# Four residual blocks on eight images: x(1) loaded when x(0) is there, other orders in the first and last cycle, and x2 of images 0 and 7 copied from SBUF to C's windows

## What is computed

```
x = x + conv3x3(gn(x), w0) + b0          # A, zero padding
x = x + inverse(gn(x))                   # B
x = x + circular_conv3x3(gn(x), w2)      # C, wraps around in rows and columns
x = x + mask * conv3x3(gn(x), K)         # D, last row and column of the conv are 0

def inverse(W):                          # each channel is a 128 x 128 matrix
    X = W^T / (norm1 * norminf)          # the norms are maxima over the channels of an image
    for _ in range(5):                   # Newton-Schulz
        X = X @ (2 I - W @ X)
    return X
```

## Time and profile before

| | |
|---|---|
| median of 3 runs | 651.18 us (649.93 to 652.49) |
| profiled execution, its own time | 653.21 us |
| its span | 651.1 us, 12738 instructions |
| TensorE busy, matmuls / weight loads | 595.6 us (91%) / 505.6 us (78%) |
| VectorE | 509.9 us (78%) |
| ScalarE | 357.9 us (55%) |
| GpSimd | 192.0 us (29%) |
| mean granted TensorE clock | 0.974 of full |
| DMA | 69.07 MB, 106 GB/s on average |
| share of the chain that ended last: TensorE, VectorE | 80%, 8% |

### The profile page before, as it was taken

How to read it: one execution, slowest core, us unless ns; L and a number is a source line. 1 busy time by engine, 2 the same in 40 slices (tenths; PEclk the granted TensorE clock), 3 DMA queues, 4 the chain that set the end, 5 groups by cost and what they waited for, 6 DMA issues and landing times.

```text
span 651.1 us, 12738 instructions
## 1 busy us (share of the span) xinstructions
PE 595.6 (91%) x3880; PEld 505.6 (78%) x3880; DVE 509.9 (78%) x1477; ACT 357.9 (55%) x713; POOL 192.0 (29%) x283
## 2 busy tenths in 40 slices
PE   0596996999999999999999999999999999988775
PEld 0475985798879787889779787889879887987454
DVE  2877587789887898888887898798887888598660
ACT  0354524575567557575558547566558447643452
POOL 6020440054214240154114241254014041440303
PEclk9998997999999999999999999999999999997888
DMA  6154113227334344236414544426414324400432
GB/s 171 49 152 119 50 51 120 63 51 226 94 91 93 116 137 143 82 82 182 153 54 99 145 137 119 112 64 194 131 52 104 107 81 134 108 33 34 134 107 65
DMA packets 85859, 69.07 MB, mean 106 GB/s; under 512 B 7886, under 2 KB 77166, under 8 KB 84910
## 3 DMA queue, kind: packets, MB, share of 16 engines
q1 hardware_dynamic: 80768, 63.21, 34.3%
q0 software_dynamic: 3456, 4.63, 2.7%
q10 hardware_dynamic: 1598, 0.77, 0.5%
HBM read 31.84 MB, written 25.30 MB: 88 GB/s over the span
## 4 chain that ended last, share of the span: by engine, by line
PE 80%; DVE 8%; DMA 3%; ACT 3%; SPq 3%; issue 2%; POOL 0%; DVEq 0%; ACTq 0%
PE conv_ps L628 40%; PE R_ps L775 17%; PE V_ps L775 16%; PE R_ps L736 4%; SPq L276 2%; DMA win_A<-x 2%; PE conv_ps L753 1%; PE V_ps L753 1%; DMA x<-x_dram 1%; DVE st L563 1%; DVE bn_A L444 1%; ACT DN L907 1%; ACT d_C L543 1%; DVE VT L1062 1%; PE row_ps L769 0%
## 5 line engine op out<-in xcount | busy, mean ns | idle before, releaser
L628 PE MATMUL conv_ps<-d_C,w_C 128*96 128x512 f32 (+1 forms) x486 | 112.6, 389 | 7.8 <-POOL d_C L674 6.9
L628 PEld LDWEIGHTS conv_ps<-d_C,w_C 128*96 128x96 f32 x486 | 76.0, 166 | 39.2 <-issue 10.2
L628 PE MATMUL conv_ps<-d_A,w_D 128*96 128x512 f32 (+1 forms) x432 | 102.2, 387 | 2.0 <-DVE w_D L496 2.0
L1254 POOL TENSOR_TENSOR RC<-RY 128x512 f32<-128x512 f32 x32 | 40.4, 1283 | 171.3 <-ACT RY L891 171.3
L628 PE MATMUL conv_ps<-d_A,w_A 128*96 128x512 f32 (+1 forms) x378 | 88.7, 390 | 2.0 <-DVE w_A L496 2.0
L628 PEld LDWEIGHTS conv_ps<-d_A,w_D 128*96 128x96 f32 x432 | 66.2, 164 | 25.4 <-DVE w_D L496 2.1
L674 POOL TENSOR_TENSOR d_C<-d_C,ones_all 128x8 fp32r<-128x8 f32 (+1 forms) x96 | 26.0, 302 | 190.1 <-DVE d_C L506 190.0
L628 PEld LDWEIGHTS conv_ps<-d_A,w_A 128*96 128x96 f32 x378 | 59.4, 167 | 24.2 <-DVE w_A L496 2.1
L663 ACT ACTIVATE out_C<-conv_ps,col_C 96x512 f32<-96x512 f32 (+1 forms) x48 | 31.1, 648 | 60.0 <-PE conv_ps L628 60.0
L663 ACT ACTIVATE out_D<-conv_ps,col_D 96x508 f32<-96x508 f32 (+1 forms) x48 | 30.8, 641 | 59.1 <-PE conv_ps L628 57.6
L775 PE MATMUL R_ps<-RY 128*128 128x128 f32 x512 | 62.1, 277 | 0.5 <-ACT RY L891 0.5
(11 more groups left out here) (179 smaller groups left out, 1170.2 us busy)
## 6 DMA issues: line engine op xcount, KB each, us to landing
win_C<-rows_dram SPq DMA_DIRECT2D x40, 256.0 KB, 3.9
x<-x_dram SPq DMA_DIRECT2D x16, 512.0 KB, 4.6
rows_dram<-x SPq DMA_DIRECT2D x32, 256.0 KB
y<-out_D SPq DMA_DIRECT2D x160, 48.0 KB
win_D<-out_C SPq DMA_DIRECT2D x7, 1056.0 KB, 6.8
x_dram<-out_A SPq DMA_DIRECT2D x35, 192.0 KB, 2.9
win_A<-x SPq DMA_DIRECT2D x79, 64.0 KB
win_A<-x POOLq DMA_DIRECT2D x56, 64.0 KB, 2.9
```

The costliest lines, as they stand in the source:

```text
L628: return pe.matmul(conv_ps[g % 2][0:OP, 0:kn, :], c.w[:, wp, dx * OP:(dx + 1) * OP], c.d[:, dp, k0:k0 + kn, dx:dx + W], start=(wp, dp, dx) ...
L1254: pool.tensor_tensor(RC[s][:, :, :], RY[s][:, :, :], RY2[s][:, :, :], ALU.add).then_inc(s_half, 1)
```

## The change

- **Start.** Image 0's windows go over the queues as groups 0 and 3 (SP), 1 and 4 (ScalarE's), 2 and 5 (GpSimd's), with four semaphores of their own, so that VectorE's statistics begin with groups 0 to 2. All three queues then wait until image 0 has landed (`x0_loaded`) before they load image 1. The bias is loaded ahead of that wait; the taps of C and D come behind it.
- **x2 of images 0 and 7.** `windows_from_x2` takes the place of stores, edge rows and loads in cycles 0 and 7. Each of the 22 windows is one DMA from 8 (at the edges 7) partitions of x2 to 128 (112) of `win_C`, and two more DMAs bring the wrapped rows. SP issues the first half of each group and GpSimd the second, 12 DMAs each, when the whole of x2 is there. They have a semaphore per group and queue, for which `high_parts` waits.
- **First cycle.** `dve_round_2_first` takes all statistics of x1(1) ahead of `dve_z_z2`, half of x2's and B's mean between the steps, the second part of `win_stats_1` of image 2 behind C's mean; TensorE's `row_mean` and `row_var` of B move ahead.
- **Last cycle.** `dve_round_2_last` takes half of x2's statistics and D's `win_stats_2` ahead of the steps of round 2, couples `dve_z_z2` with the steps chunk by chunk, and puts D's weights ahead of the last step and C's mean between D's low parts. On TensorE and ScalarE C's mean, variance and square root come one group of D earlier. GpSimd waits for `cD.s_stat` before `pool_powers` of round 2.
- `keep_x1` and the first x2 step wait for `cC.s_dl` in place of `s_xs`. The middle cycles' order is that of before (`dve_round_2`); counts of `s_xs`, `s_first_C` and `cC.s_win` start one image later.

```diff
@@ -265,6 +269,8 @@
             second = isinstance(b, int) and b == 1
             win = (cA1 if second else cA).win
             by_sp, by_pool = (s_xsp1, s_xpool1) if second else (s_xsp, cA.s_win)
+            if isinstance(b, int) and b == 0:
+                by_sp = by_pool = (s_x0_pool if g in (2, 5) else s_x0)[g // 3]
             if second:
                 eng.wait_ge(s_zero, 2)
             else:
@@ -309,6 +315,33 @@
             cs = slice(NMAT * ch, NMAT * (ch + 1))
             sp.dma_start(rows_dram[1:H + 1, cs, :], x2[:, cs, :]).then_inc(s_xs, 16)
+        def at_an_end(b):
+            return isinstance(b, int) and b in (0, B - 1)
+        def near_count(g, by_sp):
+            return (3 if g == 0 else 1 if g == NG - 1 else 2) if by_sp else 2
+        def windows_from_x2(eng, b, by_sp):
+            if b == 0:
+                eng.wait_ge(cA.s_dl, 2 * NG)
+            else:
+                eng.wait_ge(cC.s_dl, NG * b)
+            eng.wait_ge(s_x2, NCHK * (b + 1))
+            for g in range(NG):
+                k0, kn = SPLIT_G[g]
+                done = (s_near_sp if by_sp else s_near_pool)[g]
+                for k in range(k0, k0 + kn // 2) if by_sp else range(k0 + kn // 2, k0 + kn):
+                    h0 = window_row(k)
+                    lo, hi = max(h0, 0), min(h0 + WIN, H)
+                    eng.dma_start(cC.win[(lo - h0) * C:(hi - h0) * C, k, :], x2[lo:hi, :, :]).then_inc(done, 16)
+                    if k == 0:
+                        eng.dma_start(cC.win[0:C, k, :], x2[H - 1:H, :, :]).then_inc(done, 16)
+                    if k == NBLK - 1:
+                        eng.dma_start(cC.win[(WIN - 1) * C:, k, :], x2[0:1, :, :]).then_inc(done, 16)
         def store_x2_edges(sp, b):
             sp.wait_ge(s_x2, at(NCHK, b, NCHK))
@@ -319,9 +352,7 @@
             if g == 0:
                 wait(sp, cC.s_dl, at(NG, b))
-                if isinstance(b, int) and b == 0:
-                    sp.wait_ge(cA.s_dl, 2 * NG)
-                sp.wait_ge(s_xs, at(16 * n_xs, b, 16 * n_xs))
+                sp.wait_ge(s_xs, at(16 * n_xs, b - 1, 16 * n_xs))
             k0, kn = SPLIT_G[g]
             regular = min(kn, NBLK - 1 - k0)
...
@@ -531,10 +567,13 @@
                     act.wait_ge(cA.s_acc, 2 * NG)
                 if c is cA:
                     wait(act, cD.s_acc, at(NG, b - 2))
-            if c is cC and g < 2:
-                act.wait_ge(s_first_C[g], at(16, b, 16))
-            if c is cC and g == 2:
-                act.wait_ge(c.s_win, at(16 * n_x2, b, 16 * n_x2))
+            if c is cC and at_an_end(b):
+                act.wait_ge(s_near_sp[g], 16 * near_count(g, True) * (1 if b == 0 else 2))
+                act.wait_ge(s_near_pool[g], 16 * near_count(g, False) * (1 if b == 0 else 2))
+            elif c is cC and g < 2:
+                act.wait_ge(s_first_C[g], at(16, b - 1, 16))
+            elif c is cC and g == 2:
+                act.wait_ge(c.s_win, at(16 * n_x2, b - 1, 16 * n_x2))
             if c is not cC and g in (0, NG - 1):
                 e, k = (0, 0) if g == 0 else (1, NBLK - 1)
                 act.activation(c.win[:, k, :], c.win[:, k, :], ACT.Identity, bias=col(c, ADD + e),
@@ -714,16 +753,18 @@
             if not prev:
                 store_x1(sp, i + 1)
                 load_x1(sp, i + 1)
-            store_x2(sp, i, 0)
-            store_x2(sp, i, 1)
-            if nxt and prev:
+            if at_an_end(i):
+                windows_from_x2(sp, i, True)
+            else:
+                store_x2(sp, i, 0)
+                store_x2(sp, i, 1)
                 store_x1(sp, i + 1)
                 load_x1(sp, i + 1)
-            store_x2(sp, i, 2)
-            store_x2(sp, i, 3)
-            store_x2_edges(sp, i)
-            for g in range(NG):
-                load_x2(sp, i, g)
+                store_x2(sp, i, 2)
+                store_x2(sp, i, 3)
+                store_x2_edges(sp, i)
+                for g in range(NG):
+                    load_x2(sp, i, g)
             if prev:
                 store_y(sp, i - 1, range(NG if nxt else NG - 2))
@@ -836,20 +878,22 @@
             pe_apply(pe, i, 1, 1)
             if prev and nxt:
                 conv_group(pe, cD, i - 1, 0, beside)
+            if not prev:
+                row_mean(pe, st, sB_bn, sB_sum, i + 1)
             pe_apply(pe, i, 1, 2)
             pe_apply(pe, i, 1, 3)
             for g in range(1 if nxt else 0, NG if nxt else NG - 2):
                 if prev:
                     conv_group(pe, cD, i - 1, g, beside)
-                if nxt and g == 2:
+                if middle and g == 2:
                     row_mean(pe, st, sB_bn, sB_sum, i + 1)
-                if nxt and g == 2 and not prev:
+                if not prev and g == 1:
                     row_var(pe, st, dev, sB_bn, sB_sum, i + 1)
-                if prev and g == (3 if nxt else 2):
+                if prev and g == (3 if nxt else 1):
                     row_mean(pe, st_C, sC_bn, sC_sum, i)
-                if nxt and g == 4 and prev:
+                if middle and g == 4:
                     row_var(pe, st, dev, sB_bn, sB_sum, i + 1)
-                if prev and g == (4 if nxt else 3):
+                if prev and g == (4 if nxt else 2):
                     row_var(pe, st_C, dev_C, sC_bn, sC_sum, i)
         def pe_end(pe):
@@ -913,7 +957,7 @@
         def keep_x1(act, b):
-            wait(act, s_xs, at(16 * n_xs, b))
+            wait(act, cC.s_dl, at(NG, b))
             c1 = NMAT * NCHK // 2
             act.activation(x2[:, c1:C, :], x1[:, c1:C, :], ACT.Copy).then_inc(s_keep, 1)
@@ -962,11 +1006,10 @@
                     act_DN(act, i + 1, 3)
                 if nxt and g == 4:
                     act_sqrt(act, sB_ve, sB_sd, tB[:, 3, :], tB[:, 2, :], i + 1)
-                if prev and g == (4 if nxt else 3):
+                if prev and g == (4 if nxt else 2):
                     act_sqrt(act, sC_ve, sC_sd, col(cC, SD), col(cC, VE), i)
-                if not nxt and g == 3:
-                    high_parts(act, cC, i, 0)
-                    high_parts(act, cC, i, 1)
+                if not nxt and g >= 2:
+                    high_parts(act, cC, i, g - 2)
             if middle:
                 high_parts(act, cC, i, 0)
                 high_parts(act, cC, i, 1)
...
@@ -1164,58 +1211,88 @@
...
+            link_B = Chain(dve, s_chainB, perB, i + 1)
+            link = Chain(dve, s_chainC, perRC, i)
+            if middle:
+                dve_round_2(dve, i, nxt2, link_B, link)
+            elif nxt:
+                dve_round_2_first(dve, i, link_B, link)
+            else:
+                dve_round_2_last(dve, i, link)
+            dve_rows_C_var(dve, link, i)
+            dve_rows_C_weights(dve, link, i)
+            low_parts(dve, cC, i, 1)
...
+        def dve_round_2_first(dve, i, link_B, link):
+            dve_step(dve, i, 1, 0, 0)
+            dve_step(dve, i, 1, 0, 1)
+            dve.wait_ge(s_x1, 2 * 16 * n_x1)
+            row_stats_1(dve, x1, st, sB_bn, 0, G)
+            dve_z_z2(dve, i, 1)
+            dve_step(dve, i, 1, 1, 0)
+            dve_step(dve, i, 1, 1, 1)
+            row_stats_1(dve, x2, st_C, sC_bn, 0, G // 2)
+            dve_step(dve, i, 1, 2, 0)
+            dve_step(dve, i, 1, 2, 1)
+            row_stats_2(dve, link_B, st, dev, sB_bn, sB_sum, tB, i + 1)
+            dve_step(dve, i, 1, 3, 0)
+            dve_step(dve, i, 1, 3, 1)
+            dve.wait_ge(s_x2, at(NCHK, i, NCHK))
+            row_stats_1(dve, x2, st_C, sC_bn, G // 2, G)
+            row_stats_3(dve, link_B, i + 1)
+            dve_rows_C_mean(dve, link, i)
+            win_stats_1(dve, cA, i + 2, 1)
+        def dve_round_2_last(dve, i, link):
+            row_stats_1(dve, x2, st_C, sC_bn, 0, G // 2)
+            win_stats_2(dve, cD, i - 1)
+            dve_step(dve, i, 1, 0, 0)
+            dve_step(dve, i, 1, 0, 1)
+            for s in range(2):
+                dve_z_z2_of(dve, i, 1, s)
+                dve_step(dve, i, 1, 1, s)
+            dve_step(dve, i, 1, 2, 0)
+            dve_step(dve, i, 1, 2, 1)
+            win_stats_3(dve, cD, i - 1)
+            win_weights(dve, cD, i - 1, True)
+            dve_step(dve, i, 1, 3, 0)
+            dve_step(dve, i, 1, 3, 1)
+            low_parts(dve, cD, i - 1, 1)
+            dve.wait_ge(s_x2, at(NCHK, i, NCHK))
+            row_stats_1(dve, x2, st_C, sC_bn, G // 2, G)
+            low_parts(dve, cD, i - 1, 2)
+            dve_rows_C_mean(dve, link, i)
+            low_parts(dve, cD, i - 1, 3)
         def dve_end(dve):
             for g in range(2, NG):
@@ -1274,7 +1351,11 @@
             if prev and nxt2:
                 for g in POOL_X:
                     load_x(pool, i + 2, g)
+            if not nxt:
+                pool.wait_ge(cD.s_stat, at(2, i - 1, 2))
             pool_powers(pool, i, 1)
+            if at_an_end(i):
+                windows_from_x2(pool, i, False)
             pool_pads(pool, i, 0, 1)
@@ -1294,17 +1375,25 @@
```

(16 more changed lines are left out.)

74 lines of the change are left out of this document (30 added, 44 removed).

## The result

The changed kernel takes **645.82 us** (median of 9 runs, 644.50 to 648.11) against 652.39 us of the kernel before on the same chips (9 runs, 649.60 to 652.90). The ratio is 0.9915, with a 95% interval of 0.9897 to 0.9934: 0.85% faster. The forecast was 638.3 us with a range of 633 to 645. The sign was right, the gain was half of what was forecast, and the time lies 0.8 us above the range. The profiled execution of the changed kernel took 645.82 us itself, with a span of 643.9 us (653.21 and 651.1 before).

A forecast was written before the change was run, and what follows sets the result against it. TensorE was taken to bound the middle, with waits binding at the start, the end of the first cycle and the last cycle; gains of 4.2 + 3.3 + 5.4 = 12.9 us took 651.18 to 638.3 us, range 633 to 645.

The forecast's parts named there:

- the price of the 24 transfers: Window copies in first and last cycles: 0.3 to 0.5 us each; nothing lost in the first, SP issues 8.9 us.
- rival (a): Windows of C: copies from neighbouring partitions queue at 1.2 us each, making the kernel slower, 661 us; chance 0.06.
- The start: Image 0's loading: the step after the statistics' group sum moves from 20.5 to 16.3, 4.2 us earlier (2.2 to 5.4).
- rival (b): Start: its gain is mostly a new wait, taps at 18.3 or later or image 1 late; 640.5 us, chance 0.10.
- First cycle: End of the first cycle: reordered statistics start C's convolution at 107.7, not 111.03, 3.3 us earlier (1.5 to 4.5).
- The half clock: C's convolution in the first cycle: TensorE's half clock stays, as the idle time ahead is as long.
- Last cycle, orders: Last cycle: short small steps and new orders bring D's first output at 629.4, not 634.81; 5.4 us (3 to 6.5).
- The weights of D: Last cycle, VectorE: just behind GpSimd's last addition, they could be blocked once more, for up to 1.2 us.
- Rival (d): Last cycle: small steps stay long beside GpSimd's additions or descriptors; it gives 2 to 3 us, 641 us; chance 0.07.
- Rival (c): Start and first cycle: their gains don't pass through and only the last cycle counts; 645.8 us, chance 0.07.

## Why the prediction was half right

**The step that failed** is the price of the 24 transfers. I had bounds of 0.3 and 1.7 us per window and took 0.3 to 0.5, nearer to the stream, "since those 64 KB shared the engines with larger transfers". So I cost the copies at nothing in the first cycle and at 8.9 us of SP's time in the last. Measured: 24 copies are issued from 588.29 on and the last has landed at 603.30 when ScalarE takes it, 15.0 us or 0.62 us each with two queues in flight, and 1.18 us each on SP's queue, which is held for 13.3 us. The bounds themselves held. The fault was the choice within them, and the rows that it leant on. The 223 GB/s of the lower bound are loads from DRAM into 128 partitions. The 313 GB/s that I held against rival (a), as "rows of 512 bytes out of SBUF", I misread: most of it is loads from DRAM as well. The loads of `win_C` are issued from 601.69 to 605.3 and take about 4.2 us to land, so they are landing from 606 to 608; y's stores alone, a few us later, move 64 GB/s (second line, in the order of the earlier trace rows):

```profile
601.69 3.13 SPq L331 DMA_DIRECT2D win_C<-rows_dram  x6
```

```profile
614.00:616.00 2.00, 2.00 (x10) 1.43 (x9) 0.56 (x1) 0.68 (x1) 0.14 (x1) 1.00 0.24 64
```

What stood in question was how few, and how neighbouring, the partitions are that feed one transfer. The rows of before held no copy of that kind, so the distance between the bounds was the honest answer, and this term had to reach 0.6 us. By my own price of 2 us for that the time would have been 640.3 us, still within the range; the rest is the next point.

**That price was also too small.** At 0.62 us I had 2 us in the last cycle; it was about 5 (645.82 against 640.64), and about 2 in the first, where I had none. I had counted the windows' landing alone, up to ScalarE's first output of C. The second path is SP's time. I took 0.74 us per issue, 8.9 in all, from loads whose queue never filled. Here SP holds its queue for 4.4 us more than that, and y of image 6 and the windows of D stand behind it in order: D's windows are issued at 615.23, and with DRAM at 607.15. GpSimd's twelve took 7.3 us, as I had worked out.

**Rival (a)** named this mechanism and its direction, but gave 661 us by 1.2 us per window one after another. SP's queue takes about 1.2 us per copy while GpSimd's goes on beside it, and so half of it came. With its deciding point at 1.0 us it could say nothing about 0.6.

**The start**: forecast 4.2 us (bounds 2.2 to 5.4). The step moved by 3.5 us in the traces and the kernel by 2.3 us in the medians. The last window of image 0 still takes 5.40 us to land and so SP passes its wait at 12.8, not at 11.3. And the start of before varies by up to 1.5 us from trace to trace, so what I subtracted from the median was in part this one execution's. The wait for the taps, rival (b)'s first half, is there as forecast, but they landed at 17.04 and not at 18.3 or later; image 1 never was late. That the start alone gave about the 2 us of rival (b) is not by its mechanism.

**First cycle**: DN was forecast at 92.0 (96.2 less the start's 4.2) and came at 91.75, the square root at 99.4 and came at 98.83. These steps held. C's convolution came at 104.46 for 103.5, behind 2.02 us of waiting for windows. At the first mark 5.3 us are left of 6.6; with DRAM at both ends it is 6.1 of 6.2 (546.24 to 540.13, and 111.03 to 104.87). The difference is about what TensorE stands ahead of C's groups 2 and 3, 0.60 us before 110.84 and 0.58 before 113.88, where it does not stand with DRAM. Both times it waits for a low part that stood behind VectorE's sums for B; that the late windows put it there is likely, and not shown. The half clock at the start of this convolution stayed, as forecast.

**Last cycle, orders**: the sum was forecast 5.4 us. By the part of the span behind the first mark it is 7.6 us with DRAM (104.9 to 97.3 us), 7.8 with the orders alone (97.1), and 2.0 with the copies. The steps are right in their places: V at 577.04 (forecast 584.6 less 7.5), the products behind it without a wait and at the short time, none of the small steps of D's mean over 0.23 us. The weights of D, which I had said could be blocked once more, were not: they take 0.52 and 0.31 us from 584.99, behind GpSimd's last addition, which ends at 584.10. Rival (d) is out: with the wait removed the steps are long again and 3 us of the last cycle are lost (105.9 for 102.9 us). Rival (c) gave 645.8 us, the measured time to the digit, and that is chance: by (c) nothing of the start and the first cycle is left and the last cycle gives 5.4 us, where the traces have 5.3 us at the first mark and 2.0 behind it. The runs with the start and the orders alone show that both reach the first mark.

In sum the forecast of 638.3 us is the time of this kernel without its copies, 638.86 us. In part that is luck: it got there with a start that was sized too large by 1 to 2 us and orders of the last cycle too small by 2.

## What to carry to other kernels

Price a DMA from the partitions that it reads, not from its bytes: a row of the trace stands for it only if it reads as few, and as neighbouring, partitions. A transfer that drains slower than it is issued costs twice, at its reader and on its queue; so list what stands behind it there, and give the issue the price of the drain. Where one wait of a microsecond keeps a GpSimd addition off a chain of tiny VectorE steps, take it.

## What the hardware showed that was not expected

- Two rows of offset decide a copy's rate: 32 KB from four neighbouring partitions of SBUF take 1.01 to 1.04 us per copy from partition 4k and 0.69 to 0.82 from 4k + 2, on the same queue in the same shape.
- The way through DRAM was the faster one: with DRAM at both ends x2 is complete at 587.3, SP is through with its stores and seven loads at 594.0 (3.14 us for six of the loads), and all windows are there at 598.11. The 24 copies inside SBUF start from an x2 at 588.2, hold SP until 601.59, and have landed at 603.30. In the 16 us of the copies the engines moved 93 GB/s, in the 11 us of the way through DRAM 195, as the two tables of stages show (busy us of PE PEld DVE ACT POOL, granted clock, DMA share, GB/s; changed kernel, then DRAM at both ends):

```profile
588.00:604.00 16.00, 13.25 (x51) 8.28 (x49) 10.16 (x30) 7.19 (x12) 8.65 (x20) 0.89 0.53 93
```

```profile
587.00:598.00 11.00, 8.00 (x36) 5.16 (x35) 8.74 (x28) 4.97 (x10) 1.44 (x4) 1.00 0.65 195
```

- An issue on SP's queue grows when the transfers ahead of it drain slowly: up to 2.20 us for one in the last cycle, where the shortest is 0.60. GpSimd's issues of the same copies stay at 0.59 to 0.71 us. Why only SP's grow, no run here tells.
